# Moving the bf16 cast of the expert weights from a DMA to ScalarE, and re-laying a scratch tensor, in a mixture-of-experts layer

## The reference

```python
x = _layernorm(x + attn(x))          # linear attention, 16 heads of 64, elu(.)+1 features
x = _layernorm(x + ffn(x))

# attention
q = elu(x @ Wq + bq) + 1;  k = elu(x @ Wk + bk) + 1;  v = x @ Wv + bv
kv   = einsum('bhsd,bhse->bhde', k, v)
attn = einsum('bhsd,bhde->bhse', q, kv)
out  = sigmoid(x @ Wg + bg) * attn @ Wo + bo

# ffn: 16 experts, inner width 512, 4 chosen of the 2 best of 4 groups
c[t, e] = softmax(x @ gate_w.T)[t, e] if e is chosen for t, else 0
h1 = einsum('td,edi->tei', x, w1);  h3 = einsum('td,edi->tei', x, w3)
y  = einsum('tei,eid,te->td', silu(h1) * h3, w2, c)
z  = silu(x @ ws1) * (x @ ws3) @ ws2
return y + z
```

## Time and profile before

| | us |
|---|---|
| median of two runs | 7340.86 |
| the two runs | 7121.68 and 7560.04 |
| the profiled execution | 6725.16 |
| its span on the slowest core (4) | 6723.5 |
| spans of the eight cores | 6678.2 to 6723.5 |
| mean granted TensorE clock, cores 0 to 3 and 4 to 7 (median) | 0.923 and 0.916 |

### The profile page before, as it was taken

How to read it: one execution, slowest core, us unless ns; L and a number is a source line. 1 busy time by engine, 2 the same in 40 slices (tenths; PEclk the granted TensorE clock), 3 DMA queues, 4 the chain that set the end, 5 groups by cost and what they waited for, 6 DMA issues and landing times.

```text
span 6723.5 us, 66848 instructions; the slowest of 8 cores (6678.2 to 6723.5 us)
## 1 busy us (share of the span) xinstructions
PE 5743.7 (85%) x27750; PEld 2752.0 (41%) x27750; DVE 1725.1 (26%) x2472; ACT 718.0 (11%) x1150; POOL 1145.6 (17%) x619
## 2 busy tenths in 40 slices
PE   4884777866999999999997683999999999999494
PEld 2442555643444444444443331444444444444141
DVE  2221333322222222222221122322222222222012
ACT  1110222210000000000001100000000000000101
POOL 0001110113221122122111102212212211220200
PEclk9887888877999999999998896999999999999786
DMA  2012110014322222233220103323222322320201
GB/s 73 22 38 75 32 38 25 33 42 118 88 80 68 68 78 81 59 78 82 63 57 32 47 26 113 103 60 85 79 59 76 81 69 67 84 76 1 72 0 47
DMA packets 151642, 416.61 MB, mean 62 GB/s; under 512 B 11664, under 2 KB 20128, under 8 KB 151216
## 3 DMA queue, kind: packets, MB, share of 16 engines
q1 hardware_dynamic: 102688, 253.91, 11.5%
q0 software_dynamic: 40720, 141.67, 9.5%
q10 hardware_dynamic: 7936, 16.78, 0.8%
HBM read 282.28 MB, written 25.17 MB: 46 GB/s over the span
## 4 chain that ended last, share of the span: by engine, by line
PE 81%; DMA 6%; DVE 6%; POOL 2%; ACT 2%; issue 2%; DVEq 0%; SPq 0%; ACTq 0%; POOLq 0%
PE pb L264 26%; PE pb L266 26%; PE pb L267 26%; DMA PW<-ws 1%; POOL PW L1073 1%; DVE PM L1031 1%; DMA PW<-PW 1%; DMA PS<-h_scr 1%; DMA PW<-w 1%; PE pb L955 1%; POOL PW L793 1%; ACT PW L1070 1%; DMA PA<-Wv 1%; PE pb L681 0%; DVE PM L1038 0%
## 5 line engine op out<-in xcount | busy, mean ns | idle before, releaser
L264 PE MATMUL pb<-PA,PW 128*128 128x512 bf16 (+1 forms) x5632 | 2053.3, 365 | 227.2 <-POOL PW L1073 188.3
L266 PE MATMUL pb<-PA,PW 128*128 128x512 bf16 (+1 forms) x5632 | 2052.6, 364 | 0.0
L267 PE MATMUL pb<-PA,PW 128*128 128x512 bf16 (+1 forms) x5632 | 2051.7, 364 | 0.0
L264 PE MATMUL pb<-PW,PM 128*128 128x512 bf16 x2304 | 895.1, 389 | 90.7 <-DVE PM L1038 58.8
L793 POOL TENSOR_TENSOR PW<-PW 128x2048 bf16<-128x2048 f32 x192 | 785.9, 4093 | 738.5 <-DMA PW<-PW 738.5
L264 PEld LDWEIGHTS pb<-PA,PW 128*128 128x128 bf16 x5632 | 557.2, 99 | 827.1 <-issue 297.7
L266 PE MATMUL pb<-PW,PM 128*128 128x512 bf16 x2304 | 895.5, 389 | 0.0
L267 PE MATMUL pb<-PW,PM 128*128 128x512 bf16 x2304 | 894.9, 388 | 0.0
L1026 DVE TENSOR_TENSOR PM<-pb,PM 128x512 f32<-128x512 f32 x256 | 177.1, 692 | 2499.6 <-PE pb L267 2499.6
L267 PEld LDWEIGHTS pb<-PA,PW 128*128 128x128 bf16 x5632 | 557.6, 99 | 570.4 <-issue 36.8
L266 PEld LDWEIGHTS pb<-PA,PW 128*128 128x128 bf16 x5632 | 557.0, 99 | 563.6 <-issue 34.3
(11 more groups left out here) (162 smaller groups left out, 2434.6 us busy)
## 6 DMA issues: line engine op xcount, KB each, us to landing
PW<-w SPq DMA_DIRECT2D x192, 1024.0 KB, 5.3
PW<-PW POOLq DMA_DIRECT2D x196, 512.0 KB, 4.2
PW<-ws SPq DMA_DIRECT2D x24, 1024.0 KB, 5.0
PA<-x SPq DMA_DIRECT2D x28, 512.0 KB, 3.7
h_scr<-PA POOLq DMA_DIRECT2D x16, 512.0 KB, 3.0
PS<-h_scr POOLq DMA_DIRECT2D x16, 512.0 KB, 4.8
out<-PM POOLq DMA_DIRECT2D x16, 512.0 KB, 2.9
PW<-Wk SPq DMA_DIRECT2D x8, 512.0 KB, 4.6
```

What stands on the lines that cost most here:

```text
L264: Sd.pe(lambda e: e.matmul(bk_ap, sh, mh, start=first, stop=False), waits=waits0, want=False)
L266: Sd.pe(lambda e: e.matmul(bk_ap, sh, ml, start=False, stop=False), want=False)
L267: return Sd.pe(lambda e: e.matmul(bk_ap, sl, mh, start=False, stop=last), want=want)
```

## The change

It does two things. In `load_split_slot` the high part is made by a copy on ScalarE, with the same waits, where a DMA of GpSimd's queue made it; the subtraction on GpSimd stays, and now waits for ScalarE. This is emitted at the same place as before. And `hth_scr` and `htl_scr` have the shape [4, 8, 128, 512] in place of [8, 128, 2048]: stage B writes its pieces of 128 x 256 there, and each read of 128 x 512 now takes one contiguous block.

```diff
@@ -109,8 +109,8 @@
     aux_h = nc.dram_tensor("aux", [128, 2304], F32, kind="ExternalInput").ap()
     out_h = nc.dram_tensor("out", [S, D], F32, kind="ExternalOutput").ap()
     h_scr = nc.dram_tensor("h_scr", [S, D], F32, kind="Internal").ap()
-    hth_scr = nc.dram_tensor("hth_scr", [8, 128, S], BF16, kind="Internal").ap()
-    htl_scr = nc.dram_tensor("htl_scr", [8, 128, S], BF16, kind="Internal").ap()
+    hth_scr = nc.dram_tensor("hth_scr", [4, 8, 128, 512], BF16, kind="Internal").ap()
+    htl_scr = nc.dram_tensor("htl_scr", [4, 8, 128, 512], BF16, kind="Internal").ap()
 
     Sd = Sched()
     for nm in ("PE", "VE", "SE", "GP", "GPD", "LDI", "LDB", "LDO", "XA0", "XA1",
@@ -695,11 +695,11 @@
                 sq_guard = [htr_evs[-1], hw_now]
             for c in range(8):
                 Sd.dma("gp", lambda e, c=c, cc=cc: e.dma_start(
-                    out=hth_scr[c, :, cc * 256:(cc + 1) * 256],
+                    out=hth_scr[cc // 2, c, :, (cc % 2) * 256:(cc % 2) * 256 + 256],
                     in_=hTb_hi[:, c * 256:(c + 1) * 256]),
                     waits=[sq_guard[0]], inc="HTW")
                 hTb_guard = Sd.dma("gp", lambda e, c=c, cc=cc: e.dma_start(
-                    out=htl_scr[c, :, cc * 256:(cc + 1) * 256],
+                    out=htl_scr[cc // 2, c, :, (cc % 2) * 256:(cc % 2) * 256 + 256],
                     in_=hTb_lo[:, c * 256:(c + 1) * 256]),
                     inc="HTW")
 
@@ -788,8 +788,8 @@
                     waits=stage_free_m, inc="SWL")
                 hi_ap = slot_hi(kind, par)[:, half * 2048:(half + 1) * 2048]
                 lo_ap = slot_lo(kind, par)[:, half * 2048:(half + 1) * 2048]
-                ev_hi = Sd.dma("gp", lambda e, hi_ap=hi_ap: e.dma_start(
-                    out=hi_ap, in_=wstage), waits=[ev_l, slot_free[kind][par]], inc="GPD")
+                ev_hi = Sd.se(lambda e, hi_ap=hi_ap: e.copy(
+                    out=hi_ap, in_=wstage), waits=[ev_l, slot_free[kind][par]])
                 ev_lo = Sd.add("gp", lambda e, hi_ap=hi_ap, lo_ap=lo_ap: e.tensor_tensor(
                     out=lo_ap, in0=wstage, in1=hi_ap, op=ALU.subtract),
                     waits=[ev_hi], inc="GP")
@@ -811,11 +811,11 @@
                 for c in range(8):
                     ev_hi_t = Sd.dma("se", lambda e, c=c, hh=hh, tg=tg: e.dma_start(
                         out=hTm_hi[:, c * 1024 + tg * 512: c * 1024 + tg * 512 + 512],
-                        in_=hth_scr[c, :, hh * 1024 + tg * 512: hh * 1024 + tg * 512 + 512]),
+                        in_=hth_scr[hh * 2 + tg, c]),
                         waits=(g_se if c == 0 else []), inc="HT2")
                     ev_lo_t = Sd.dma("sy", lambda e, c=c, hh=hh, tg=tg: e.dma_start(
                         out=hTm_lo[:, c * 1024 + tg * 512: c * 1024 + tg * 512 + 512],
-                        in_=htl_scr[c, :, hh * 1024 + tg * 512: hh * 1024 + tg * 512 + 512]),
+                        in_=htl_scr[hh * 2 + tg, c]),
                         waits=(g_sy if c == 0 else []), inc="HT")
                 ht_chain_se = ev_hi_t
                 ht_chain_sy = ev_lo_t
```

## The result

The changed kernel is slower: 1.158 times the time before, with a 95% interval of 1.154 to 1.162. Its median over 12 executions is 8214.6 us (7748.4 to 8679.5), against 7118.6 us (6691.5 to 7587.6) of 10 executions of the kernel before. In part of the executions of either kernel the TensorEs of one die, or of both, get a lower clock and the time is up to 13% longer; the medians hold these executions, the ratios and what follows leave them out. The profiled execution took 7770.3 us, 1045.1 more than that of before.

The account below looks back on a forecast made before the run. TensorE, 85% busy, was taken to set the pace. From 6725.2 us, 30 borders at +37.2 (+1116), expert 0 +4 and layout 0 gave 7845; plus 250 for lower clock, 8095 us, range 7700 to 8520.

Parts of the forecast that it names:

- The mechanism: Expert borders: six ScalarE copies wait for loads ahead of the first Silu, TensorE waiting some 5, 16 and 13 us.
- L1031 near 0.69 us: VectorE in the experts: sign that L1031 no longer meets GpSimd's subtractions; 3.31 us before, 2.6 saved per expert.
- A: Expert borders: ScalarE holds nothing up, copies run in its idle time; 6670 us (-0.8%); chance 0.02.
- B: Expert borders: only the weights set the pace, Silu of column 0 free; 6.8 us less each, 7641 us; chance 0.04.
- C: Expert borders: clock stays low through h1 and h3 of column 1; 8.1 us more each, 8088 us; chance 0.06.
- D: Experts: full limiter, clock 0.8 in every dense stretch; 7845 + 829 = 8674 us; chance 0.07.
- The chain: Border's six load-copy-subtraction steps: copy 6 ends 60.3 us after T0, the end of the previous expert's last cast.
- The restart: TensorE at h1 of column 1 behind the border's gap: starts at half clock, 2.1 us lost.
- The rest of the expert: From h1 of column 1 to the end of the expert's last cast: 103.6 us.
- The sum: Whole kernel on the profiled execution's terms: 6725.2 + 1116 + 4 + 0 = 7845 us.
- How runs lie about the sum: Median run above the profiled execution from lower clock: half of 505 us taken, 250, giving 8095 us.
- Expert 0 and the layout: Expert 0: -3.5 us first half, +7.1 second, together +4; scratch layout: 0, bounds -35 to +35 us.

Follow-up runs that it names:

- block_early: Changed kernel, but the next expert's six loads emitted as one block behind the last cast of the first token group: 167.4 us per expert, 7817.9 us.
- spread: Changed kernel, but the next expert's six loads emitted one by one behind the casts of the expert before: ratio 0.984 to the kernel before.
- silu_first: Changed kernel, but w2's two loads emitted behind the Silu of token group 0, column 0: 159.5 us per expert, 7570.1 us.
- layout_only: Kernel before with only the scratch tensors in the new shape, cast still a GpSimd-queue DMA: 129.6 us per expert, span 6701.8 us.

## Why the prediction was right, step by step

**The mechanism** was right: copies from the last L1034 on, the Silu right behind the sixth, and three TensorE waits, "some 5, 16 and 13 us", measured 5.25, 15.31 and 10.62. One sign given ahead was wrong: "L1031 near 0.69 us". At each border the L1031 of column 0 took some 4 us (4.08 in the row in the last section), since it follows the Silu behind copy 6 and so meets the sixth subtraction, which the prediction's own times had from T0 + 60.5 to T0 + 64.6. It cost nothing, as h1 and h3 of column 1 stand between it and the matmuls that want it. Where the prediction counted on it, at the last column, L1031 did take 0.69. `block_early` and `spread` show that it is the place in the queue and not ScalarE's load.

**Rivals.** A (ScalarE holds nothing up) fell with the result; `spread` shows that its time is real where the order is made for it, at 0.984 even below A's 0.992. B (the weights set the pace) fell with `silu_first`. C (the clock stays low) fell: ten slow matmuls at this restart, 7 to 15 at the 30 borders. D (full limiter in the experts) isn't what the profiled execution shows: in 1765:1860, between two borders, the clock was 1.00 on each of the eight cores. Its time, 8674 us, is that of the longest execution, 8679.5, of which there is no trace.

**The sizes.** The chain: T0 + 58.6 at the end of copy 6 at this border and T0 + 59.1 on average, where the prediction had T0 + 60.3. I had added 5 x 0.3 us because the experts' loads land later than the shared expert's; the steps were (1752.81 - 1696.07) / 5 = 11.35 us here, 11.46 on average over the kernel, hardly longer than the shared stage's 11.4, and the load's median fell from 5.3 to 5.2 with the cast DMAs gone. The restart: 1.9 us here and 2.1 on average, against 2.1. The rest of the expert: 1755.35 to 1860.80 is 105.45, less 1.9 is 103.55, against 103.6. A mean border cost 165.3 - 129.5 = 35.8 us, not 37.2, nearly all of it by the chain: 30 x 1.4 = 42 us too much in the sum.

**The sum** on the profiled execution was 7845, measured 7770.3. Of the 75 us, 42 are the borders. Another 38 (with some 5 the other way around expert 0) are in the execution that I counted from: behind expert 15's first Silu of the second half, core 4 took 6723.5 - 6113.1 = 610.4 us before and the changed kernel's core 2 took 7768.3 - 7195.5 = 572.8. There before's clock was 0.86, and here it is 0.99 (windows, columns as in rows 2):

```profile
7440.00:7640.00 200.00, 197.42 (x907) 89.03 (x906) 34.36 (x50) 15.79 (x26) 0.00 (x0) 0.99 0.00 1
```

I had that row and used it for how runs lie, and not for what the reference execution held.

**How runs lie about the sum** is the term that was mis-sized. I let half of the surplus come back, 250 us, for a median of 8095, "as the gaps lower the load". The changed kernel's median lies 444 us above its profiled execution, and that of before, over ten executions, 393 above its own. But neither surplus is a fixed size: three sets of executions of the kernel before have medians of 6781.2 (11 executions), 7118.6 (10) and 7275.1 us (11), and the two of the ten that I had to go by 7340.9. So the runs show neither that the gaps lower the surplus nor that they don't. The forecast of 8095 came within 120 us of 8214.6 since the sum was 75 us too high and the surplus 194 too low, and that is luck. What sets the lower clock wasn't studied here. The Trainium skill ("TensorE: Matmul & The Clock Gate", section "Seeing it yourself") says that a die goes to 13/16 of the clock once three of its cores run dense matmuls. The traces agree with the level, 0.81 on core 4 of the kernel before in 6440:6600, and not with the condition, since the clock was 1.00 with all eight cores at work (D above).

**Expert 0 and the layout.** The prediction had -3.5 us for expert 0 of the first half and +7.1 for that of the second. From the end of the router's Exp to the Silu of column 2 it took 87.4 us before (core 4) and 83.0 after (core 2) in the first half, -4.4, and 76.8 and 83.6 in the second, +6.8. The layout's 0 was right (`layout_only`).

## What to carry to other kernels

Ask of an instruction that moves to another engine's queue what stands behind it there, and how long it will wait for its own inputs: six copies of 1.9 us on an engine that is 11% busy cost 35.8 us per expert, since each brought its load's wait with it. Emit such an instruction where its input has landed already, one at a time between the urgent ones; the same copies then made the kernel 1.6% faster in place of 15.8% slower. And look for old blocks of the same kind, such as the shared expert's 12 loads: they showed both the fault's price ahead of time and the next gain.

## What the runs showed of the hardware

A wait of TensorE can cost more than its length. After one of 10.62 us it began again at half clock, 1.9 us more, and so it was at each of the 30 borders (7 to 15 slow matmuls). Even behind a wait of 2.73 us (rows at 1958.37 above) it lost 1.3 us more, and behind 19 of 27 such short waits the clock was halved for some time. In the kernel before this hid in experts that seemed full, and it is why `spread` gained 3.2 us per expert where the waits themselves were 2.1.

VectorE's operation with two inputs from SBUF stood still while GpSimd subtracted. In `silu_first` L1040 ran from 1746.33 to 1750.46, the subtraction from 1745.86 to 1749.92, so VectorE's 0.69 us came behind it. In the changed kernel L1031 at the border has the same (VectorE's timeline):

```profile
1755.38 4.08 DVE L1031 TENSOR_TENSOR PM<-PM 128x512 f32<-128x512 f32 x1 [9.77 <-ACT PM L1022]
```

The Trainium skill ("SBUF — State Buffer", section "SBUF: two separate sides") says that a VectorE operation with two inputs from SBUF and a GpSimd operation that reads SBUF lock one port pair against each other, each for its whole instruction. The trace agrees: in the kernel before all 46 L1031 that began during a subtraction took longer, up to 4.57 us, and the other 210 took 0.69. L1026, which reads one input from PSUM, took 691 to 693 ns in both kernels, also when it began during a subtraction.
